# A two-layer decoder: GpSimd's weight split in 256-column pieces, shared weights loaded a stage earlier, first waits moved to first uses

## The reference

```python
x = _layernorm(x + _L0_attn_ref(x, ...))        # a recurrence over time, and its channel mix
x = _layernorm(x + _L0_xattn_ref(x, ctx, ctx, mask, ...))
x = _layernorm(x + _L0_ffn_ref(x, router_w, w_gate, w_up, w_down, sw_gate, sw_up, sw_down))
x = _layernorm(x + _L1_attn_ref(x, ...))
x = _layernorm(x + _L1_xattn_ref(x, ctx, ctx, ...))
x = _layernorm(x + _L1_ffn_ref(x, ...))         # 32 experts, top 4
```

```python
logits = x_flat @ router_w.T
top_vals, top_idx = jax.lax.top_k(logits, 2)    # of 7 experts
combine = ...softmax(top_vals) at top_idx...
mixed = einsum("end,ne->nd", swiglu(x_flat, w_gate, w_up, w_down), combine)
mixed = mixed + mean(swiglu(x_flat, sw_gate, sw_up, sw_down), axis=0)
```

## Time and profile before

| | |
|---|---|
| median of 3 runs | 3280.51 us (3275.11 to 3284.24) |
| the profiled execution | 3279.13 us |
| its span, first to last instruction | 3277.1 us |
| mean granted clock of TensorE | 0.876 |
| PE busy | 2504.0 us (76%) |
| PEld busy | 2091.4 us (64%) |
| DVE busy | 2118.1 us (65%) |
| ACT busy | 1096.4 us (33%) |
| POOL busy | 817.2 us (25%) |
| cross attention 0 | about 581 to 1082 us |
| first mixture | about 1083 to 2118 us |
| cross attention 1 | from about 2413 us |

### The profile page before, as it was taken

One profiled execution on the slowest core, in us unless ns is written; L12 is line 12 of the kernel. 1 busy time (PEld: TensorE's weight loads), 2 busy tenths in 40 slices (PEclk: granted clock), 3 DMA queues, 4 the chain that ended last, 5 costly groups with the idle time before them and its releaser, 6 DMA issues. The chain is left out here.

```text
span 3277.1 us, 52248 instructions
## 1 busy us (share of the span) xinstructions
PE 2504.0 (76%) x17441; PEld 2091.4 (64%) x17442; DVE 2118.1 (65%) x5466; ACT 1096.4 (33%) x1952; POOL 817.2 (25%) x932
## 2 busy tenths in 40 slices
PE   4787877599999699987989989866748999837400
PEld 3666666366665599987889889855635666537400
DVE  5888886367676576667666665555545888745554
ACT  2343433255555222211111112122635555425400
POOL 0000000011111243123121120054111444442574
PEclk8999998699999799988989999988878998868755
DMA  1010001454441300021011010111026566327887
GB/s 52 20 35 19 22 19 55 81 78 72 71 69 21 128 26 32 25 97 58 26 64 64 26 64 26 51 56 38 0 51 85 110 92 83 47 73 207 209 122 91
DMA packets 201928, 210.32 MB, mean 64 GB/s; under 512 B 39889, under 2 KB 188152, under 8 KB 201808
## 3 DMA queue, kind: packets, MB, share of 16 engines
q1 hardware_dynamic: 166352, 142.53, 20.6%
q0 software_dynamic: 18432, 36.94, 6.6%
q10 hardware_dynamic: 17024, 29.36, 2.5%
HBM read 103.42 MB, written 67.90 MB: 52 GB/s over the span
## 5 line engine op out<-in xcount | busy, mean ns | idle before, releaser
L1516 PE MATMUL m_gu<-m_x_hi,m_w_hi 128*128 128x256 f32 x1632 | 466.1, 286 | 27.8 <-DVE m_x_lo L1582 17.3
L1516 PE MATMUL m_gu<-m_x_hi,m_w_lo 128*128 128x256 f32 x1632 | 461.6, 283 | 0.0
L1516 PE MATMUL m_gu<-m_x_lo,m_w_hi 128*128 128x256 f32 x1632 | 460.8, 282 | 0.0
L1554 ACT ACTIVATE m_sg<-m_gu 128x256 f32<-128x256 f32 x408 | 157.0, 385 | 752.0 <-PE m_gu L1516 752.0
L1588 DVE TENSOR_TENSOR m_h<-m_sg,m_gu 128x256 f32<-128x256 f32 x408 | 171.6, 421 | 309.8 <-ACT m_sg L1554 307.9
L1057 ACT ACTIVATE x_pt<-x_ps 128x1024 f32<-128x1024 f32 x256 | 262.3, 1025 | 224.9 <-PE x_ps L889 220.9
L1516 PEld LDWEIGHTS m_gu<-m_x_hi,m_w_hi 128*128 128x128 f32 x1632 | 313.2, 192 | 32.5 <-DVE m_x_lo L1582 17.7
L1516 PEld LDWEIGHTS m_gu<-m_x_hi,m_w_lo 128*128 128x128 f32 x1632 | 313.3, 192 | 0.0
L1516 PEld LDWEIGHTS m_gu<-m_x_lo,m_w_hi 128*128 128x128 f32 x1632 | 313.0, 192 | 0.0
L1505 PE MATMUL m_yp<-m_w_hi,m_h_hi 128*128 128x256 f32 x816 | 244.6, 300 | 78.7 <-DVE m_h_lo L1590 78.6
L1157 DVE CUSTOM_DVE_ANT_0 x_ps<-x_ps,x_mb 128x256 f32<-128x256 f32 x512 | 201.7, 456 | 116.3 <-PE x_ps L889 116.2
(11 more groups left out here) (303 smaller groups left out, 5586.5 us busy)
## 6 DMA issues: line engine op xcount, KB each, us to landing
m_x<-xs SPq DMA_DIRECT2D x68, 256.0 KB, 2.8
ys<-m_y SPq DMA_DIRECT2D x67, 256.0 KB, 2.2
x_qpack<-x_qh SPq DMA_DIRECT2D x128, 128.0 KB
x_kpack<-x_kh SPq DMA_DIRECT2D x128, 128.0 KB
xs<-zero SPq DMA_DIRECT2D x8, 1024.0 KB, 5.2
x_cx<-in_ctx SPq DMA_DIRECT2D x32, 256.0 KB, 4.6
x_qpack<-x_ql SPq DMA_DIRECT2D x64, 128.0 KB
x_kpack<-x_kl SPq DMA_DIRECT2D x64, 128.0 KB
```

Of the source, the lines that this page charges most:

```text
L1516: ins = pe.matmul(gu[:, m % 4, n, :], wp[n][:, c, m * P:m * P + P], xp_[:, c, :], start=(c == 0 and k == 0), stop=(c == KC - 1 and k == 2))
L1554: act.activation(sg[:, m % 4, :], gu[:, m % 4, 0, :], ACT.Silu).then_inc(silu_ready, 1)
```

## The change

1. In the first mixture POOL's casts and subtractions of 2048 columns become 8 instructions of 256 columns each; the counts waited for on `hi_ready` and `w_ready` are eight times as large. ACT's and DVE's split of the shared weights stays whole.
2. `raw` and its three semaphores are allocated around cross attention 0 and the first mixture. SP issues the load of the shared weights in cross attention 0 at p = 8, ahead of that period's `pack_maxima`; ACT's load at the start of the mixture is gone.
3. In both cross attentions, `kpack` is filled by POOL in three pieces, with a semaphore `ones_ready` that SP waits for ahead of the key packs of the first three sequences; the waits at the head of PE's and POOL's programs go to the parts that first need them; DVE turns the key weights before it fills `vp` and `nmx`; the router's weights wait for the fill of `wg` alone, and `route` waits for a new `wg_ready`.

```diff
@@ xattn_stage, sync
-                sp.wait_ge(preset, 4)
+                sp.wait_ge(preset, 1)
                 sp.dma_start(wg[:, :, 0:experts], col(d["L0_ffn_router_w"])).then_inc(w_loaded, 16)
...
             def pack_queries(n):
-                if n == 0:
-                    sp.wait_ge(preset, 2)
...
             def pack_keys(n):
+                if n < PACKS:
+                    sp.wait_ge(ones_ready, n + 1)
                 sp.wait_ge(kh_ready, n + 1)
...
             for p in PERIODS:
+                if masked and p == B // 2:
+                    load_raw(sp, st, d, 0, st.shared_loaded)
                 at(p - 1, pack_maxima)
@@ xattn_stage, gpsimd
             def add_bias(n):
+                if n == 0:
+                    pool.wait_ge(w_loaded, 16 * 4)
...
-            pool.wait_ge(w_loaded, 16 * 4)
+            for u in range(PACKS):
+                pool.memset(kpack[:, u].bitcast(F32), 1.0).then_inc(ones_ready, 1)
@@ xattn_stage, tensor
-            pe.wait_ge(w_loaded, 16 * 4)
-            pe.wait_ge(w_turned, 2)
-            pe.wait_ge(preset, 4)
-            pe.wait_ge(mask_ready, 2 * TB if masked else 1)
...
             def project_queries(n):
+                if n == 0:
+                    pe.wait_ge(w_turned, 2)
...
             def project_values(n):
+                if n == 0:
+                    pe.wait_ge(w_loaded, 16 * 4)
...
             def key_scores(n, g):
+                if masked and n == 0 and g == 0:
+                    pe.wait_ge(mask_ready, 2 * TB)
...
             def route(n):
                 pe.wait_ge(nT_ready, n + 1)
+                if n == 0:
+                    pe.wait_ge(wg_ready, 1)
@@ xattn_stage, vector
-            dve.memset(kpack[:].bitcast(F32), 1.0).then_inc(preset, 1)
-            dve.memset(vp[:, :, :, :, DH:32], 0.0).then_inc(preset, 1)
-            dve.memset(nmx[:], 0.0).then_inc(preset, 1)
             dve.memset(wg[:], 0.0).then_inc(preset, 1)
-            dve.wait_ge(preset, 4)
-            n_ones = s.mark(dve.memset(vp[:, :, :, :, DH:DH + 1], 1.0))
             dve.wait_ge(raw_loaded, 16 * 3)
             dve.tensor_copy(wqk[:, 1]..., wqk_raw[:, 1]...).then_inc(w_turned, 1)
+            s.mark(dve.memset(vp[:, :, :, :, DH:32], 0.0))
+            s.mark(dve.memset(nmx[:], 0.0))
+            s.after(s.n)
+            s.mark(dve.memset(vp[:, :, :, :, DH:DH + 1], 1.0))
             dve.wait_ge(w_loaded, 16 * 4)
...
+                dve.wait_ge(mask_ready, 2 * TB)
+                dve.sem_inc(wg_ready, 1)
             else:
-                s.after(n_ones)
-                dve.tensor_copy(wg[:], wg_bf[:]).then_inc(mask_ready, 1)
+                dve.wait_ge(preset, 1)
+                s.after(s.n)
+                dve.tensor_copy(wg[:], wg_bf[:]).then_inc(wg_ready, 1)
@@ moe0_stage
+        PIECES = [slice(S * n, S * n + S) for n in range(FC * D // S)]
...
             def split_hi(b, n):
-                pool.tensor_copy(w_hi[:, b, n], raw[:, n]).then_inc(hi_ready, 1)
+                for piece in PIECES:
+                    pool.tensor_copy(w_hi[:, b, n, piece], raw[:, n, piece]).then_inc(hi_ready, 1)
 
             def split_lo(e, b, n):
-                pool.wait_ge(hi_ready, 3 * e + n + 1)
-                pool.tensor_tensor(w_lo[:, b, n], raw[:, n], w_hi[:, b, n].bitcast(F32), ALU.subtract).then_inc(w_ready, 1)
+                pool.wait_ge(hi_ready, len(PIECES) * (3 * e + n + 1))
+                for piece in PIECES:
+                    pool.tensor_tensor(w_lo[:, b, n, piece], raw[:, n, piece], w_hi[:, b, n, piece].bitcast(F32),
+                                       ALU.subtract).then_inc(w_ready, 1)
...
-                pe.wait_ge(w_ready, 3 * (e + 1))
+                pe.wait_ge(w_ready, len(PIECES) * 3 * (e + 1))
@@ moe0_stage, scalar
-            load_raw(act, 0, shared_loaded)
             for n in range(3):
-                act.wait_ge(shared_loaded[n], 16)
+                act.wait_ge(st.shared_loaded[n], 16)
                 act.activation(w_hi[:, 0, n], raw[:, n], ACT.Copy).then_inc(first_hi, 1)
@@ decoder
-        for stage in STAGES:
-            stage(nc, st, d)
-            st.end_stage(nc)
+        run([setup_stage, rwkv_stage])
+        with nc.sbuf_tensor("raw", [P, 3, FC * D], F32) as st.raw:
+            run([xattn0_stage, moe0_stage])
+        run([attn1_stage, xattn1_stage])
         moe1_stage(nc, st, d, out)
```

More of the change, by code:

```diff
@@ L1327, in _, with load_raw @@
                 dve.wait_ge(counted, 18)
+def load_raw(eng, st, d, w, loaded):
+    for n, name in enumerate(("L0_ffn_w_gate", "L0_ffn_w_up", "L0_ffn_w_down")):
+        src = d[name].rearrange("e (k p) n -> p e k n", p=P)
+        eng.dma_start(st.raw[:, n].rearrange("p (k n) -> p k n", k=src.shape[2]),
+                      src[:, bass.ds(w, 1)].squeeze(1)).then_inc(loaded[n], 16)
 def moe0_stage(nc, st, d):
@@ L2288, in decoder, with run @@
         st.xsh, st.ysh = dram("xsh", [N, D]), dram("ysh", [N, D])
-        for stage in STAGES:
-            stage(nc, st, d)
-            st.end_stage(nc)
+        st.shared_loaded = [ctx.enter_context(nc.semaphore(f"shared_loaded{n}")) for n in range(3)]
+        def run(stages):
+            for stage in stages:
+                stage(nc, st, d)
+                st.end_stage(nc)
+        run([setup_stage, rwkv_stage])
+        with nc.sbuf_tensor("raw", [P, 3, FC * D], F32) as st.raw:
+            run([xattn0_stage, moe0_stage])
+        run([attn1_stage, xattn1_stage])
         moe1_stage(nc, st, d, out)
```

17 lines of the change are left out of this document (5 added, 12 removed).

## The result

| | before | after |
|---|---|---|
| median, the kernels run beside each other | 3277.81 us (4 runs) | 3159.32 us (3153.64 to 3166.68, 4 runs) |
| profiled execution, its span | 3279.13, 3277.1 us | 3163.98, 3162.3 us |
| mean granted clock of TensorE | 0.876 | 0.890 |

The ratio is 0.9638 (0.9608 to 0.9669): 118.5 us less, where 107.1 had been worked out from 3280.51. 3159.3 lies 14.1 us under the predicted time, and 1.7 us under the lower end of the range. Of the 14.1, 8.0 are in the profiled pair (115.1 in place of 107.1), 4.7 are what the profiled execution of after lay above its median, 1.4 the same of before. The direction and the mechanism hold; sizes were off.

A forecast was written before the change was run, and what follows sets the result against it. PE's program was taken to set the end of the first mixture, with POOL's holding up of DVE on top. Gains 85.7 + 4.0 + 9.4 + 5.6 + 3.4 - 1.0 = 107.1 took 3280.5 to 3173.4 us; range 3161 to 3191.

The forecast's parts named there:

- A: First mixture, routed experts: splitting in pieces of 256 columns gains 85.7 us, bounds 70.7 and 93.5.
- B: First mixture, three shared tiles: the same pieces cut 4.6 us of waits to 0.6, gaining 4.0, bounds 3 and 5.4.
- D: Cross attention 0: first waits moved, so the first projection and all behind it come 5.6 us earlier; bounds 3 and 6.5.
- E: Cross attention 1: the same moved waits gain 3.4 us, bounds 1 and 4.
- C: Start of the first mixture: shared weights loaded a stage ahead, PE starts 9.4 us earlier without a stall; bounds 3 and 9.8.
- F: Cross attention 0: the moved load delays sequence 7's maxima and key scores, costing 1.0 us; bounds 0 and -6.
- 0.2 for the hand-over: Routed splits: DVE's step for a hidden block takes 0.45 us plus twice a piece with about 0.2 added.
- the 17 us that I had worked out as the worst of it: Routed split: each of 48 pieces waits one DVE operation of 0.36 us, so the split would end at 57 us.
- PE waiting for the transposes of tile 1: Start of the first mixture: listed among the signs that would show the forecast wrong.
- rival 1: Start of the first mixture: shared tile 0 runs into missing rows, gain 6.4 us less, 3180; chance 0.18.
- Rival 3: Splits: DVE gets no turn at piece borders, h_hi held through the 26.6 us run, about 3330; chance 0.04.
- Rivals 2 and 4: Splits: 2, pieces too long or POOL's stretched, 21 us less, 3194, chance 0.09; 4, pieces change nothing, 3263, chance 0.03.

The follow-up runs named there:

- e0: The changed kernel run again beside the three parts alone: median 3154.72 us, ratio 0.9653 to the kernel before.
- e1: The kernel before with only the waits and fills of the cross attentions moved: 3252.24 us, ratio 0.9957 to the kernel before.
- g2: The changed kernel with subtractions in pieces of 128 columns, casts still 256: ratio 0.9649 to the kernel before, tiles 917.7 us.
- h2: The changed kernel with casts of the first two weights in 128 columns, the third's in 256, subtractions 256: ratio 0.9946 to the kernel before, tiles 1016.8 us.
- e2: The kernel before with only the shared weights loaded a stage ahead, splits whole: 3262.37 us, ratio 0.9985 to the kernel before.
- f1: The changed kernel with the gathered rows' buffer zeroed a stage before cross attention 0, POOL's wait dropped: ratio 0.9630 to the kernel before, tiles 918.3 us.
- g1: The changed kernel with casts in pieces of 128 columns, subtractions still 256: ratio 0.9957 to the kernel before, tiles 1024.8 us.
- h3: The changed kernel with casts of the first two weights in 256 columns, the third's in 128, subtractions 256: ratio 0.9944 to the kernel before, tiles 1028.9 us.
- f3: The changed kernel with casts and subtractions both in pieces of 128 columns: ratio 0.9721 to the kernel before, tiles 961.2 us.
- e3: The kernel before with only POOL's pieces of 256 columns: 3170.47 us, ratio 0.9708 to the kernel before.
- f4: The changed kernel with PE's mask wait put back ahead of its first transpose in cross attention 0: ratio 0.9669 to the kernel before.

## Why the prediction was right, and where it was wrong

**What failed** is the size of terms, and in one of them the overlap. Measured by the parts alone, A and B gave 96.7 us in place of 89.7, D and E 15.0 in place of 9.0, C and F 4.8 in place of 8.4. In the prediction's own words: "I take 1.5 per split" was too much (0.9 of stall is left); "All behind it (packs, first scores) hangs on that chain and moves along" left out what came on top of the shift; and "no stall" for tile 1 was wrong, which hid a part of the others. By its own rows D was 593.99 - 588.3 = 5.7 and E 2424.57 - 2421.1 = 3.5, 0.1 more each than was put down.

Against the profiled pair, 114.8 us of span:

| step | predicted | measured | |
|---|---|---|---|
| A, routed splits | 85.7 | 89.1 | 5.6 us left in place of 9.0 |
| B, shared tiles | 4.0 | 5.6 | all of the excess went |
| C, loads ahead | 9.4 | 9.8 - 3.5 = 6.3 | the rows of tile 1, as in rival 1; 4.1 to 6.6 over 11 profiles |
| D and F, cross attention 0 | 4.6 | 5.3 (8.3 in e0, e1) | 6 to 7 by the first scores, then 0 to 3; the end behind the last maxima moves by 1.5 |
| E, cross attention 1 | 3.4 | 10.9 | 3.8 as predicted; 2.6 between the maxima; 4.5 in the end |
| the rest | 0 | -2.3 | last stage |

**A and B** hold as a mechanism: DVE gets in at a border and is held for about one piece. The size failed at "the two held operations cost up to 0.5 us there in the cast phase, 1.1 in the other", of which I took 1.5. Beside the casts DVE's pair took 0.50 + 0.50 us, not twice 0.59, and cost nothing; beside the subtractions 0.38 + 0.84, not twice 0.92, as only one of the two operations was held. The second tile of each of six experts takes 0.4 to 0.9 us over 17.6, 4.6 in all; the other 1.0 us of the 5.6 is spread over the expert starts and third tiles. Of the added "0.2 for the hand-over" 0.06 (0.84 beside a piece of 0.78) to 0.11 (0.50 beside 0.39) was there. `g2` bears it out: with subtractions of 128, `h_lo` takes 0.57 us, and PE's wait for it falls to 0.7 us.

**The cost of a piece** was right for the cast (0.39) and low for the subtraction: 0.72 worked out, 0.778 measured, and 0.685 where DVE gets no turn. So DVE's turns stretch POOL by 0.09 us a piece. The Trainium skill (SBUF — State Buffer, section Who interferes with whom) has the shared port pair as an exclusive lock, so each side holds off the other; the trace agrees in kind, and the 17 us that I had worked out as the worst of it were 24 x 0.09 = 2.2 in the subtractions, and less in the casts (in `h2`, six casts beside a hold took 0.35 us each, against 0.39). My reading of before, that DVE's time is not added to POOL's, was too simple: with three long subtractions such turns are too few to be seen. It cost nothing, as the weights were still ready in time.

**C** failed at "now mostly do not; I expect them some 5 us earlier and no stall". SP issues the eight zero fills sooner (9.97 us in place of 16.35), but POOL's sends, which wait for the fills, begin 23.1 us after its first copy and not 21.0: 2.1 later, not 5 earlier. Its copy for tile 1 comes 29.9 us after the first and not 31.6, 1.7 sooner, where PE's need moved by 9.8. `e2` has the same, 23.1 and 29.7. What the prediction overlooked stands in ACT's queue: with the shared weights split sooner, `raw` is free sooner, and the load of expert 0's weights goes out 8.7 us after POOL's first copy, while the fills are being issued (1.6 to 11.5), and not at 18.4, behind them (1.6 to 17.9). Before, then after:

```profile
1084.87 16.35 SPq L1394 DMA_DIRECT2D xs<-zero  x8
1101.75 0.37 ACTq L1380 DMA_DIRECT2D m_raw<-in_L_ffn_w_gate  x1
1104.29 1.22 POOL L1453 DMA_INDIRECT xs<-m_x,m_idx  x1 [20.23 <-issue]
```
```profile
1079.42 9.97 SPq L1406 DMA_DIRECT2D xs<-zero  x8
1086.53 0.45 ACTq L1346 DMA_DIRECT2D raw<-in_L_ffn_w_gate  x1
1100.94 1.22 POOL L1468 DMA_INDIRECT xs<-m_x,m_idx  x1 [22.33 <-issue]
```

From 1087 to 1097 us the DMA engines of after are full (share 0.97 and 1.03, 319 and 354 GB/s in its two halves). So the fills still ran beside 3 MB of weights, only other ones; that this is what held them back fits the rows, but no run moved that load alone. PE then waited 2.75 us (up to 4.1 in the other profiles, with a slow second tile behind it); the rest of the 3.5 goes with a lower clock at the start (0.68 granted in the first 10 us, 0.73 in before). This is the sign "PE waiting for the transposes of tile 1" that the prediction had named, and **rival 1**'s mechanism: C fell short of 9.4 by 2.8 to 5.3 us of that rival's 6.4, hidden in the total by the terms that gave more. `f1` shows that the fills matter: without them the first tile is 4.4 us shorter.

**F** is right only by its number. `e2` has 1.8 us more in the stage, but not where the load stands: from the first to the last maxima it takes 396.5 us, as before does (396.4), PE has no gap at the key scores of sequence 7, and the maxima of sequence 7 leave as early as before. The excess is behind the last maxima, a part that takes 44.9 to 48.2 us in kernels with the load and 46.7 to 47.1 in the three without. So no cost of the load is shown.

**D** named the chain rightly: the first projection at 587.4, predicted 588.3, in a stage that now starts 0.1 sooner. Its size was a little low, because before's own chain had 13.7 us to the first projection and after's 7.2, 6.5 and not 5.6 (ACT's turn of the weights, which I had left where it was, came 0.9 us sooner), and because "All behind it ... moves along" left out the up to 2 to 3 us between scores and maxima. The doubled clock of the key and value projections, which I had not foreseen, changed nothing by the first scores, since a DMA is last there.

**E** has 3.8 us of its own in after, `e0` and `e1`; over all 15 kernels with moved waits the first maxima come 49.0 to 51.7 us after the stage's start (five of them at 49.0 to 49.3) and not 55.3, and what picks one of these stays open too. The 2 to 4 us between its maxima stand in the three profiles that can be compared with kernels that keep the waits, for a reason that stays open. The 4.5 at its end come and go.

**The range** was missed by 1.7 us, and the 2.7 us by which the median of before moved are more than that. But the sum itself was off by 11.4 us (118.5 in place of 107.1), with errors of both signs: C, put too high, made up for part of what A, D and E had too low, and that is luck. Nor did the range allow for the 2 to 7 us by which one stage differs between profiles of kernels that are alike in it, beyond "a few us for the run to run".

**Rival 3** got 0.04, and "at both borders seen in the casts DVE got in" was true of this kernel and is not a rule: with casts half as wide it happens in up to six splits of six. The Trainium skill (GPSIMD Engine Reference, section 2.1 Instruction dispatch), which I cited as leaving least room at a border, fits what `g1` shows and not what after shows; a page's rule alone would have decided neither. **Rivals 2 and 4** are out: PE waited for `h_lo` six times in the mixture, 0.8 us at most, no expert waited for its weights (though DVE's turns did stretch POOL's pieces), and 1.40, 0.84 and 0.57 us follow the pieces of 512, 256 and 128.

## What to carry to other kernels

Where GpSimd and VectorE both work from SBUF, look at how long single VectorE instructions take beside GpSimd's, and cut the long GpSimd instruction; the cost was 0.17 us a further cast and 0.13 a further subtraction ((9.37 - 5.83) / 21 and, without VectorE's turns, (16.43 - 13.70) / 21; with them (18.67 - 13.70) / 21 = 0.24), on an engine with time to spare. Then look again after every change of the size: going from 256 to 128 columns in the casts took back everything, while the same step in the subtractions gained 5 us in the tiles. And when a load is moved ahead of its wait, ask what else the first work needs; here the rows of the second tile were behind fills that could move as well. Ask too which later load the faster start sets off: here that of the next weights came forward into the fills.

## What the runs showed of the hardware that I had not expected

- A VectorE operation of 0.29 us (once one of 0.43) was held for 16.2 to 18.7 us, over the borders of all 24 GpSimd subtractions of 0.685 us, in 17 of 18 splits of `g1`, `h2` and `h3`, and once in `f3` for 14.0 us, over 37 borders; in the kernels with casts of 256 columns and more none took over 0.90 us (1.40 with subtractions of 512). Subtractions of 128 columns (0.47 us) behind casts of 256 held `h_lo` for 0.57 us and `h_hi` for 0.67 at most.
- GpSimd's own time tells which of the two holds: 0.685 us a piece of 256 where VectorE gets no turn, 0.778 where it does.
- In cross attention 0, starting four small transposes some 12 us earlier went with a clock at 2.4 GHz for the projections of keys and values, 13 and 17 us after the stage's start, in 13 profiles of 14; with the wait kept (before, `e2`, `e3`, `f4`) they ran at 1.2 GHz in all four. The one of 14 that stayed slow reached its first scores just as soon. The wait is not all there is to it: in cross attention 1 the same projections took 1.96 to 1.99 us with the wait kept (before, `e2`, `e3`) and 3.75 in one of 15 with it moved (`f3`).
- Loads that one engine's queue issues sooner can meet the fills of another: with expert 0's load issued 9.8 us earlier in the stage, eight fills were issued within 9.97 us in place of 16.35, and the sends that wait for them began 2.1 us later.
